# The expert stage moved between the two batches of an attention loop, with its rows gathered and summed by GpSimd during the second batch

## The reference, cut to what matters

```
s = attn(xn)                 # two attentions side by side, 8 heads each, on 64 features each
                             # (the second on features smoothed over time), out projection,
                             # layer norm, feed-forward 128-512-128, layer norm
# the gate: each of 4096 tokens goes to 4 of 32 experts, at most 640 rows per expert
xe  = xp[buf_tok].reshape(32, 640, 128)
h   = silu(einsum('ecd,edh->ech', xe, w1)) * einsum('ecd,edh->ech', xe, w3)
out = einsum('ech,ehd->ecd', h, w2) * buf_w[..., None]
y   = zeros(N + 1, 128).at[buf_tok].add(out)[:N]     # each token sums its up to 4 expert rows
z   = silu(xf @ sw1) * (xf @ sw3) @ sw2              # an expert that all tokens share
x   = x + s * silu(y + z)
```

## Time and profile before

| | us |
|---|---|
| time, median of 3 runs | 1940.49 (1936.45 to 1942.12) |
| span of the profiled execution | 1937.5 |
| attention, from the first exponential tile to the last matmul of unit 31 | 111.5 to 1297.06 |
| expert stage, to PE's last matmul | to 1422.1 |
| back half of layer one, to about 1690 | |
| PE busy over the span | 1748.8 (90%) |
| DVE | 1642.1 (85%) |
| ACT | 1524.2 (79%) |
| GpSimd | 524.8 (27%) |

### The profile page before, as it was taken

The page is one execution under the profiler, slowest core; times in us unless marked ns, Lnnn a source line. Parts: engine busy times, 40 slices in busy tenths (PEclk is TensorE's granted clock), DMA queues, the critical chain, the costliest instruction groups (busy, mean ns, idle before and its releaser), DMA issues.

```text
span 1937.5 us, 41198 instructions
## 1 busy us (share of the span) xinstructions
PE 1748.8 (90%) x15427; PEld 673.9 (35%) x15428; DVE 1642.1 (85%) x2481; ACT 1524.2 (79%) x2889; POOL 524.8 (27%) x795
## 2 busy tenths in 40 slices
PE   6799999999999999999999999999975567899884
PEld 4322222222222222222222222238842223366553
DVE  7799999999999999999999999925446565499778
ACT  5579999999999999999999999983323456776556
POOL 2433300320002232232222221000036556033425
PEclk9899999999999999999999999999987888799897
DMA  3422221211111111111111111028852333422121
GB/s 118 162 68 80 83 71 53 83 38 32 28 35 46 41 46 53 42 43 56 41 44 55 43 58 35 11 63 235 228 164 83 96 106 101 114 71 57 37 71 44
DMA packets 151356, 142.14 MB, mean 73 GB/s; under 512 B 38986, under 2 KB 130125, under 8 KB 151010
## 3 DMA queue, kind: packets, MB, share of 16 engines
q1 hardware_dynamic: 142818, 122.36, 21.5%
q0 software_dynamic: 8352, 17.29, 3.1%
HBM read 76.60 MB, written 60.03 MB: 71 GB/s over the span
## 4 chain that ended last, share of the span: by engine, by line
PE 68%; ACT 11%; DVE 9%; issue 5%; POOL 3%; another core or an unknown queue 2%; DMA 2%; SPq 0%; DVEq 0%; ACTq 0%; POOLq 0%
PE PS L1901 27%; PE PS L1929 17%; PE PS L1885 10%; ACT probs L1270 6%; PE PS L1979 3%; POOL VP L1741 2%; PE PS L1964 2%; DVE hst L1041 1%; PE PS L1956 1%; PE PS L2091 1%; PE PS L2028 1%; DVE VP L1018 1%; DVE VP L1026 1%; DVE YM L924 1%
## 5 line engine op out<-in xcount | busy, mean ns | idle before, releaser
L829 DVE TENSOR_REDUCE mxp<-PS 128x1 f32<-128x1024 f32 x1024 | 1171.9, 1213 | 25.2 <-PE PS L1885 19.2
L1270 ACT ACTIVATE probs<-PS 128x512 f32<-128x512 f32 x2048 | 1094.7, 597 | 64.2 <-PE PS L1929 20.6
L1901 PE MATMUL PS<-probs,VH 128*32 128x256 f32 x8192 | 642.2, 391 | 1.9 <-ACT probs L1270 0.6
L1929 PE MATMUL PS<-stacks 51*128 51x512 bf16 x2048 | 440.4, 387 | 19.6 <-ACT probs L1270 16.9
L1885 PE MATMUL PS<-stacks 48*128 48x512 bf16 x2048 | 418.6, 380 | 9.8 <-DMA stacks<-qkl_d 8.6
L1901 PEld LDWEIGHTS PS<-probs,VH 128*32 128x32 f32 x8192 | 173.0, 108 | 414.0 <-issue 235.4
L1929 PEld LDWEIGHTS PS<-stacks 51*128 51x128 bf16 x2048 | 116.4, 93 | 459.7 <-ACT probs L1270 406.9
L1741 POOL DMA_INDIRECT VP<-oe_d,ROWI x128 | 132.0, 1031 | 246.8 <-DMA oe_d<-stacks 158.8
L1631 POOL DMA_INDIRECT xe_d<-xn_s,rows_s x128 | 126.4, 987 | 216.9 <-PE PS L1901 172.5
L1609 POOL CAST spl<-nmx 128x8 bf16<-128x8 f32 x64 | 12.1, 189 | 506.4 <-DVE nmx L824 297.0
L1885 PEld LDWEIGHTS PS<-stacks 48*128 48x128 bf16 x2048 | 105.8, 95 | 25.3 <-DVE mxp L829 13.3
(11 more groups left out here) (362 smaller groups left out, 1845.6 us busy)
## 6 DMA issues: line engine op xcount, KB each, us to landing
stacks<-qkl_d SPq DMA_DIRECT2D x128, 96.0 KB
xe_d<-zt SPq DMA_DIRECT2D x16, 640.0 KB
stacks<-xe_d SPq DMA_DIRECT2D x32, 320.0 KB, 3.8
oe_d<-stacks SPq DMA_DIRECT2D x32, 320.0 KB, 3.2
stacks<-qkl_d SPq DMA_DIRECT2D x128, 64.0 KB
o_d<-SG SPq DMA_DIRECT2D x256, 32.0 KB
ews<-in_ew_dram SPq DMA_DIRECT2D x33, 192.0 KB, 2.5
stacks<-qkl_d SPq DMA_DIRECT2D x128, 32.0 KB
```

The lines of the kernel that those rows point to most:

```text
L829: v.tensor_reduce(mxp[:, n // 2, n % 2:n % 2 + 1], MXB[n % 2].rearrange("p a c -> p (a c)"), X_AX, ALU.max).then_inc(mx_done, 1)
L1270: act.activation(probs[:, at:at + 512], PS[:, bank_of(u, e), :], ACT.Exp, scale=float(1.0 / np.sqrt(np.float32(DK)))).then_inc(exp_done, 1)
L1901: mm = pe.matmul(OB[32 * jg:32 * jg + 32, c:c + 256], VH[w][:, kt, :], probs[:, at:at + 256], start=(kt < 2 and half == 0), stop=(kt >= TC ...
L1929: pe.matmul(PS[:, bank_of(u, e), :], KS[w][o:o + KROWS + 3, kt * P:(kt + 1) * P], QS[w][o:o + KROWS + 3, q0:q0 + 512], start=True, stop=Tr ...
```

## The change

Units are now taken batch by batch: unit u is head u % 16 of batch u // 16. The expert stage runs after unit 17 (`EXPERTS_AT = 18`) and the attention goes on after it. Scattering is moved to GpSimd's slots for units 12 to 19 (four tiles a slot, without the copies of the row numbers and the tokens into staging buffers). The gathers and the combining are GpSimd's, in its slots for units 21 to 31, three tiles a slot; as GpSimd's slot u waits for the weighing of unit u-3, this lies in PE's units 18 to 28. `combine` is now four groups of `tensor_tensor` on GpSimd and no longer part of DVE's order. `gate_y` runs for all eight blocks in one go ahead of the first square root. The softmax sums of batch 0 are inverted within the expert stage, those of batch 1 on DVE at step s = -1. The first two `load_attn` no longer run within the expert stage: their buffers overlay the operands of the attention, and they wait for its last weighing. The experts' buffers lie in `XNT` and `probs` instead of the operand stacks, `GB` in `S0` instead of `VP`.

```diff
+HALF = UNITS // 2
+EXPERTS_AT = HALF + 2
+SCATTER_AT, SCATTER_TILES = HALF - 4, 4
+GATHER_AT, GATHER_TILES = EXPERTS_AT + 3, 3
+CHUNK_AT = CHUNKS * (EXPERTS_AT + 1) + AHEAD
...
             for uu in range(UNITS):
                 for n in range(CHUNKS):
+                    if CHUNKS * uu + n == CHUNK_AT:
+                        expert_stage()
...
-            def combine(j):
-                v.wait_ge(ga_ld[j % 2], 64 * TB * (j // 2 + 1))
-                v.wait_ge(sh_out, NB)
-                for n in range(KTOP):
-                    for t in range(TB * j, TB * j + TB):
-                        ins = v.scalar_tensor_tensor(YM[:, t, :], GB[:, t % (2 * TB), n, :], WK[:, t, n:n + 1], YM[:, t, :], ALU.mult, ALU.add)
-                    if n < KTOP - 1:
-                        link(ins)
-                ins.then_inc(y_sum, 1)
...
                 if 0 <= s + 1 < NB:
                     attn_apply(s + 1)
+                if s == -1:
+                    for quarter in range(4):
+                        sums_inverse(1, quarter)
+                    v.wait_ge(y_sum, NT)
...
-                if s >= 0:
-                    gate_y(s)
+                if s == -2:
+                    for j in range(NB):
+                        gate_y(j)
...
+            for u in range(UNITS):
+                unit_exp(u, u % 4, u // 4, u in (EXPERTS_AT - 1, UNITS - 1))
+                if u == EXPERTS_AT - 1:
+                    turned(0, 0)
+                    repeat(act, E // 4 - 1, experts)
+                    experts(E // 4 - 1, True)
+                    act.wait_ge(hh_done, E)
+                    act.wait_ge(rl_st, 16 * NB // B)
...
+            def combine(k):
+                tiles = gather_group(k)
+                pool.wait_ge(ga_ld[k % 2], 64 * sum(len(gather_group(i)) for i in range(k % 2, k + 1, 2)))
+                rows = lambda t: GB[:, t % (2 * TB), :, :]
+                for t in tiles:
+                    ins = pool.tensor_tensor(rows(t), rows(t), WK[:, t, :].unsqueeze(2).broadcast_to([P, KTOP, D]), ALU.mult)
+                plink(ins)
+                for t in tiles:
+                    ins = pool.tensor_tensor(rows(t)[:, 0:2, :], rows(t)[:, 0:2, :], rows(t)[:, 2:4, :], ALU.add)
+                plink(ins)
+                for t in tiles:
+                    ins = pool.tensor_tensor(rows(t)[:, 0, :], rows(t)[:, 0, :], rows(t)[:, 1, :], ALU.add)
+                plink(ins)
+                for t in tiles:
+                    pool.tensor_tensor(YM[:, t, :], YM[:, t, :], rows(t)[:, 0, :], ALU.add).then_inc(y_sum, 1)
+
+            def gather(u):
+                k = u - GATHER_AT
+                first = gather_group(k)[0]
+                for t in gather_group(k):
+                    after(pool, y_sum, t + 1 - 2 * TB)
+                    for n in range(KTOP):
+                        step = KTOP * (t - first) + n
+                        if step:
+                            pool.wait_ge(pv_done, TCH * (u - 3) + step)
+                        if step == 3:
+                            largest(u - 3, 1)
+                        pool.indirect_dma_start(GB[:, t % (2 * TB), n, :], None, oe_d, bass.IndirectOffsetOnAxis(ROWI[:, t, n:n + 1], 0),
+                                                bounds_check=last_row, oob_is_err=False).then_inc(ga_ld[k % 2], 16)
+                largest(u - 2, 0)
+                if k > 0:
+                    combine(k - 1)
...
-            for i in range(2):
-                pool.wait_ge(sc_st[i], 64 * NT // 2)
-                pool.wait_ge(oes_st[i], 16 * E // 2)
-            for t in range(NT):
-                if t % TB == 0:
-                    after(pool, y_sum, t // TB)
-                for n in range(KTOP):
-                    pool.indirect_dma_start(GB[:, t % (2 * TB), n, :], None, oe_d, bass.IndirectOffsetOnAxis(ROWI[:, t, n:n + 1], 0),
-                                            bounds_check=last_row, oob_is_err=False).then_inc(ga_ld[t // TB % 2], 16)
...
+            hold(rl_st, 16 * NB // B)
+            hold(xct_st, 16)
+            hold(pv_done, TCH * UNITS)
+            load_attn(0)
+            load_attn(1)
...
++                pe.wait_ge(exp_done, EXPS * EXPERTS_AT)
+                pe.wait_ge(mx_done, chunks)
+                turn_tokens(0, 0, 0)
+                pe.wait_ge(o_evac, 2 * EXPERTS_AT)
+                repeat(pe, E // 4 - 1, experts)
...
+                pe.wait_ge(oe_out, E)
```

More of the change, by code:

```diff
@@ L174, in build @@
         zt = sb("zt", [P, 2 * D])
-        rows_s = [sb(f"rows_s{i}", [P, KTOP], mybir.dt.uint32) for i in range(2)]
-        xn_s = [sb(f"xn_s{i}", [P, D]) for i in range(2)]
         gs = sb("gs", [P, 1, NT])
@@ L1280, in unit_exp @@
                     evac(u, 0, 1)
-            def group_exp(k, last=False):
-                for w in range(4):
-                    unit_exp(4 * k + w, w, k, last and w == 3)
             act.wait_ge(xct_st, 16)
@@ L1710, in rows_step, with plain @@
                     end_rows()
-            for u in range(3, UNITS // 2):
+            def plain(u):
                 values(u)
                 largest(u - 3, 1)
-                rows_step(2 * (u - 3))
+                if u < SCATTER_AT:
+                    rows_step(2 * (u - 3))
                 largest(u - 2, 0)
-                rows_step(2 * (u - 3) + 1)
+                if u < SCATTER_AT:
+                    rows_step(2 * (u - 3) + 1)
+            for u in range(3, SCATTER_AT):
+                plain(u)
             pool.wait_ge(rows_done, 1)
@@ L1721, in _ @@
             pool.wait_ge(zero_st, 16 * (UNITS // 2 + 1))
-            for u in range(UNITS // 2, UNITS):
+            for u in range(SCATTER_AT, SCATTER_AT + NT // SCATTER_TILES):
                 values(u)
                 scatter(u)
+            for u in range(SCATTER_AT + NT // SCATTER_TILES, GATHER_AT):
+                plain(u)
+            last_row = pool.alloc_register("last_row")
+            pool.reg_mov(last_row, E * CAP)
+            for i in range(2):
+                pool.wait_ge(oes_st[i], 16 * E // 2)
+            pool.wait_ge(sc_st, 64 * NT)
+            pool.wait_ge(sh_out, NB)
+            pool.wait_ge(wk_ready, 1)
+            for u in range(GATHER_AT, GATHER_AT + GATHERS):
+                if u < UNITS:
+                    values(u)
+                gather(u)
+            combine(GATHERS - 1)
             for uu in range(UNITS - 3, UNITS):
@@ new lines, in _ @@
+            weighed, chunk = 0, CHUNKS + AHEAD
+            for u in range(UNITS):
+                w = u % 4
+                if u == EXPERTS_AT:
+                    for m in range(weighed, 2 * TCH * u):
+                        weigh(u - 1, m // 2 % TCH, (u - 1) % 4, m % 2)
+                    weighed = 2 * TCH * u
+                    expert_stage(chunk)
+                for e in range(EXPS):
+                    if e % (EXPS // 2) == 0:
+                        pe.wait_ge(m_ld[w], 64 * (u // 4) + 32 * (e // (EXPS // 2) + 1))
+                    after(pe, exp_done, EXPS * u + e - 2)
+                    o, kt, q0 = 64 * (e % 2), e // 2 % TCH, e // 2 // TCH * 1024 + e % 2 * 512
+                    pe.matmul(PS[:, bank_of(u, e), :], KS[w][o:o + KROWS + 3, kt * P:(kt + 1) * P], QS[w][o:o + KROWS + 3, q0:q0 + 512],
+                              start=True, stop=True).then_inc(sc_ready, 1)
+                    if u == RANK_UNIT and e == RANK_EXP:
+                        ranks()
+                    elif u == RANK_UNIT and e == RANK_EXP + 1:
+                        pass
+                    elif chunk < min(CHUNKS * UNITS, CHUNKS * (u + 1) + AHEAD + CHUNKS * (e + 1) // EXPS):
+                        max_chunk(chunk)
+                        chunk += 1
+                    if e == 1:
+                        pe.wait_ge(vh_ready, u + 1)
+                    for turns in range({5: 0, 7: 2}.get(e % (EXPS // 2), e % 2)):
+                        wu, pair = divmod(weighed // 2, TCH)
+                        if EXPS * wu + 4 * pair + 4 <= EXPS * u + e:
+                            weigh(wu, pair, wu % 4, weighed % 2)
+                            weighed += 1
@@ L1992, in _ @@
+            for m in range(weighed, 2 * TCH * UNITS):
+                weigh(UNITS - 1, m // 2 % TCH, 3, m % 2)
+            pe.wait_ge(exp_done, EXPS * UNITS)
+            pe.wait_ge(mx_done, CHUNKS * UNITS)
             pe.wait_ge(c_ld, 16 * NLATE)
@@ L1998, in residual @@
             def residual(j):
[L1999 removed]
+                pe.wait_ge(at_sum, j + 1)
                 after(pe, y_ready, j)
```

298 lines of the change are left out of this document (130 added, 168 removed).

## The result

The changed kernel takes 1876.03 us (median of 4 runs, 1870.69 to 1876.58), the kernel before 1938.47 in the same comparison: ratio 0.9666, 95% interval 0.9644 to 0.9688. That is 62 us less, where I had forecast 8 less and a range down to 1916. The profiled execution has a span of 1873.6 against 1937.5.

| stretch | before | after | difference | forecast |
|---|---|---|---|---|
| to the first exponential | 112.8 | 111.3 | -1.5 | 0 |
| attention and expert stage | 1309.4 | 1316.7 | +7.3 | +5.5 |
| start: to the end of attn_apply(0) | 15.1 | 26.5 | +11.4 | +9.8 |
| to x1_factors(0) | 45.7 | 26.0 | -19.7 | -16 |
| x1_factors(0) to x1_factors(7) | 183.7 | 117.6 | **-66.1** | **-7** |

What follows compares the result with a forecast made beforehand. PE, DVE and ACT were taken as full in the attention, with engines idling behind two rings in layer one's back half. Terms -23 + 9.8 + 3 + 2.5 = -7.7, say -8, gave a median of 1932.5 us, range 1916 to 1950.

Steps and rivals of the forecast that it cites:

- Combine and gathers leave the back half: Layer one's back half: moving combining and gathers out saves 23 us over its steps, bounds -16 and -41.
- Steps 3 to 7: Later back-half steps: the hidden combine gives nothing, Silu on YM leaving ACT gives 2 us.
- step 2: Back half: x1_factors(1) can start once its square root is there, 5 us gained.
- Steps 0 and 1: First two back-half steps: ff_stats(0) and attn_apply(2) start sooner, 6 and 10 us gained.
- Start: Last weighing to end of attn_apply(0): later loads and Silu with table loads add 9.8 us, between +5 and +13.
- Middle: Break in the attention after unit 17: PE drains and restarts around the expert stage, +3 us, range 1 to 6.
- GpSimd in the second half: Attention units 21 to 30: a later `largest` costs 0.25 us in each of ten slots, +2.5, bounds 0 and +20.
- Rival A: Second half of the attention: maxima come late and stall PE, costing 25 to 30 us instead of 2.5; 1957; chance 0.15.
- Rival B: Back half: steps 0 to 2 shrink by only half, 11 of 21 us, giving 1943; chance 0.20.
- Rival C: Back half: PE stays at 2.4 GHz, steps 3 to 7 shrink too, 12 us more gained, 1920; chance 0.20.

Runs made afterwards that it cites:

- e13: The kernel before, unchanged, profiled once more: ratio 1.0005 to the kernel before.
- e4: The kernel before, with GpSimd's gathers of block j waiting for the combining of block j-2, not j-1: 1889.19 us, ratio 0.9784.
- e9: The kernel before, with two GpSimd additions of 128x512 ahead of the gathers of each block but the first: ratio 1.0087.
- e10: The kernel before, gathering three experts' rows instead of four, 12 gathers per block instead of 16: ratio 0.9830.
- e11: The kernel before, with combine(s) later in DVE's program, directly ahead of ff_stats(s), gathers still waiting as before: ratio 1.0016.
- e17: The changed kernel with load_attn(0) in unit 31, the eight Silu first and ACT's wait for the attention's last stores in step 2: 0.9610 of the kernel before.
- e18: As e17, but three Silu behind the first square root and five behind the first two Relu: ratio 0.9583 to the kernel before.
- e14: The changed kernel, unchanged, run and profiled once more: ratio 0.9672 to the kernel before.
- e7: The changed kernel with load_attn(0) issued in unit 31 instead of after the last unit: ratio 0.9623 to the kernel before.
- e6: The changed kernel with gate_y's eight Silu ahead of residual_out(0) instead of behind it: ratio 0.9655 to the kernel before.
- e15: The changed kernel without the gathers and GpSimd's combining in the second half of the attention: ratio 0.9688 to the kernel before.
- e1: The kernel before, without the 128 gathers and without the combining, nothing else moved: 1846.16 us, ratio 0.9575.
- e3: The kernel before, without the gathers, DVE's combining kept in place without its wait: ratio 0.9671.
- e5: The kernel before, without combining, all 128 gathers issued back to back and DVE waiting for them once, behind the last step: ratio 0.9653.

## Why the prediction was wrong

**The step that failed is in the last line of "Combine and gathers leave the back half" ahead of the sum: "Steps 3 to 7: the combine was hidden (the 1.75 us above), so it gives nothing."** Together with step 2 it held 7 us of gain, and 66.1 came (61.0 in the second pair of profiles). What the runs showed in its place: a ring, in which the next block's gathers wait for the combining and the combining waits for the gathers, paced every step of the kernel before (e13). It was opened (e4, -41), stretched (e9, +17), shortened (e10, -33) and moved within DVE's queue (e11, nothing), and each time the steps went with it or stayed with it.

The reading error has two halves. First, the 1.75 us stood behind the combining. That ACT's square root came late too did not show that the combining was hidden, for ACT and PE follow DVE's work of the step before, which had waited in the same ring. What mattered was the wait in front of it, and this row, which I had not used, was in the same timeline:

```profile
1533.19 4.66 DVE L924 SCALAR_TENSOR_TENSOR YM<-VP,WK,YM 128x128 f32<-128x128 f32 x16 [6.65 <-DMA VP<-oe_d,ROWI]
```

In the next three blocks that wait was missing. In that profile PE's results came up to 5 us behind the end of their rows (the waits on "remote"), and steps of 29.3 hid a ring of 27.5 that was less than 1 us from pacing them too: the last gather of block 4 ended at 1559.36, its data was there 2.6 us later by e13's row, and the combining started at 1562.75. So the trace helped to mislead. e13 shows neither the lag nor the long steps. Whether they belong to that execution or to that chip is open: the runs beside it took 1935.67 to 1942.12 us, those of the comparisons on other chips (without e17's and e18's) 1921.67 to 1932.46.

Second, the size. I took the old period and subtracted the waits I could see. When a ring is opened the new period can't be less than the work per step of the fullest engine. Rows 1 had it: PE 27.4 of 50 us, so 15 us in a step of 27.3, and DVE 33.8 of 50, 18.5 with 4.7 of combining in it. That says a period of 15 us, or somewhat more in the later steps, which hold layer two's in-projection as well; 17.9 came, with PE busy 57.6 of 60 us. Windows of e13 (one step) and e14:

```profile
1504.00:1532.00 28.00, 20.50 (x62) 10.28 (x62) 16.83 (x73) 16.07 (x36) 16.40 (x16) 0.80 0.46 127
```
```profile
1500.00:1560.00 60.00, 57.61 (x205) 28.51 (x204) 42.15 (x199) 53.27 (x119) 0.00 (x0) 1.00 0.42 126
```

A later step holds some 62 of PE's rows of matmuls in both (205 x 17.94 / 60 is 61): 20.5 us of work at a mean clock of 0.80, and 17.2 (57.61 x 17.94 / 60) at 1.00. My 15 us would have been short by the later work of a step, and a later window by itself would have given too much by the clock.

Point by point:

- *Steps 0 and 1* (forecast -16): -19.7, and -20.8 in the second pair. Right, a little short.
- *Start* (+9.8): +11.4 and +11.8. The path was as described. The load took 10.8 us and not 9.0; from there on the chain was as long as forecast (15.7 us against 15.9). In e14 the load took 12.1. After the table load at 1444.88 the first Silu starts 0.02 us behind its end. The Trainium skill (ScalarE: Activation LUTs, What ACT_TABLE_LOAD costs) adds a drain of about 1.38 us to each switch; these rows don't show one, and the measurement decides. That the load was on the path e7 shows by its time and its trace; that `gate_y` was, e6 shows only in its trace (x1_factors(0) 4.3 us sooner).
- *Middle* (+3) and *GpSimd in the second half* (+2.5): together 5.5, measured 7.3 and 5.3. By e15 GpSimd's part is nothing that can be measured, which leaves the whole 5.3 of the second pair to the break, within its bounds of 1 to 6. That the sum of the two came out at 5.5 is luck: one part was too large and the other too small.
- *Rival A* did not happen. *Rival B* is refuted by e1. *Rival C* had the direction, steps 3 to 7 shrink, but at a fifth of the size and without the ring. The clock did rise, from a mean of 0.80 (e13, 1500 to 1560) to 1.00 (e14), and PE's gaps of 7 to 14 us, one in each step of e13, are gone. By the two windows above it is worth an estimated 2 to 3 us of the 10 by which a later step shrank (PE's busy time in the next e13 steps is 19.5 to 19.9 us, at 0.85 to 0.87). No run changed the clock alone.
- What moving the combining off DVE brings, apart from the ring, is the difference of e3 and e1, 18 us; and e4 reaches 41 us without moving anything. The changed kernel then pays 17 us for its start and break (5.3 + 11.8), and e1's ratio with 17 us on top is close to what it measures: 0.9575 + 0.0089 = 0.9664, measured 0.9666 and 0.9672.

## What to carry to other kernels

Where an engine waits for another that waits for it, write down the ring and its length first, and try the index that closes it: one number was worth 41 us here. When a ring or a wait is taken out, forecast the new period from the fullest engine's work per step, read from the busy times, and not from the old period less the waits you see. Take them from a window whose steps hold all the work, and mind the clock: 20.5 us of PE's work at 0.80 became 17.2 at 1.00. A wait behind an instruction does not show that the instruction was hidden; look in front of it, and in more than one execution.

## What the runs showed of the hardware that I had not expected

- 128 indirect gathers issued back to back (1.3 us each) beside PE, ACT, DVE and SP's own transfers slowed none of the steps: 17.9 us with them (e5) and without (e1).
- A gather's row ends long before its data is there: the last of a block ended at 1525.37, its data released DVE at 1527.96, 2.6 us later. The Trainium skill (Perfetto Trace Analysis, DMA Instruction, SWDGE) says that such a row ends when the descriptors are written, not when the data has moved; the trace agrees.
- GpSimd's own arithmetic does reach DVE: in e9 it adds from 1507.79 to 1509.94, and two small operations of DVE with two inputs that start in that time took 1.02 and 1.01 us in place of 0.16.
- In one execution PE's results reached the others up to 5 us behind their rows in several steps; in the later profile of the same kernel (e13) in none. I have no cause for it.
- In the first profile after, the granted clock fell to 0.58 between 1690 and 1700 with PE busy all of the time, and the rest of the kernel behind x1_factors(7) took 3.9 us longer than in e14 (275.5 and 271.6), which has a clock of 1.00 from 1670 to 1700. That the fall is the cause was not tested.
